# Normalisation of a feed-forward stage's first two groups and four of its first-layer chunks, placed within the last periods of a sixteen-head attention

## The reference

```python
# p 0, 1: x += gate * (gelu(mod(ln(x)) @ W1 + b1) @ W2 + b2), twice
# p 2:    sixteen-head attention
qkv = mod(ln(x)) @ W_qkv                                   # 256 -> 3 * 1024
attn = softmax(q @ k.T / 8)                                # per batch and head, 256 x 256
x = x + g_msa * ((attn @ v) @ W_out + b_out)
# p 3:    feed-forward, hidden width 1024
x = x + g_mlp * (gelu(mod(ln(x)) @ W1 + b1) @ W2 + b2)
# p 4, 5: masked two-direction block and feed-forward;  p 6, 7: one-head attention and feed-forward
```

## Time and profile before

| | before |
|---|---|
| median of three runs | 1716.03 us (1714.61 to 1717.41) |
| the profiled execution | 1716.76 us |
| its span in the trace | 1715.0 us |
| mean granted clock of TensorE | 0.978 |
| busy VectorE, ScalarE, POOL | 73%, 69%, 55% |
| the attention's periods | about 250 to 981 us of the span |

### The profile page before, as it was taken

One profiled execution on the slowest core, in us unless ns is written; L12 is line 12 of the kernel. 1 busy time (PEld: TensorE's weight loads), 2 busy tenths in 40 slices (PEclk: granted clock), 3 DMA queues, 4 the chain that ended last, 5 costly groups with the idle time before them and its releaser, 6 DMA issues.

```text
span 1715.0 us, 37904 instructions
## 1 busy us (share of the span) xinstructions
PE 1623.2 (95%) x13539; PEld 1472.1 (86%) x13539; DVE 1248.6 (73%) x2701; ACT 1181.6 (69%) x2944; POOL 939.8 (55%) x1135
## 2 busy tenths in 40 slices
PE   4888988999999999999999699999999999989997
PEld 2547878999999999999999599998888899979997
DVE  3766857888888888888888655556788778854442
ACT  3545657888888888888888555555766567766663
POOL 1556655666666666666666423233656578832223
PEclk7999998999999999999999899999999999999999
DMA  9223220000000000000000011101212212211111
GB/s 306 56 62 88 75 59 11 9 7 9 10 11 11 11 11 11 11 11 11 11 11 11 16 32 32 32 20 31 61 47 58 53 28 48 47 44 49 32 44 50
DMA packets 110974, 65.96 MB, mean 38 GB/s; under 512 B 81530, under 2 KB 92788, under 8 KB 110788
## 3 DMA queue, kind: packets, MB, share of 16 engines
q1 hardware_dynamic: 110788, 63.54, 14.2%
HBM read 59.06 MB, written 4.46 MB: 37 GB/s over the span
## 4 chain that ended last, share of the span: by engine, by line
PE 82%; DVE 5%; issue 3%; ACT 2%; POOL 1%; DMA 0%; POOLq 0%; DVEq 0%; ACTq 0%
PE bank L290 18%; PE bank L291 16%; PE bank L292 16%; PE bank L1143 7%; PE s_banks L1041 5%; PE bank L1117 4%; PE s_banks L290 4%; PE s_banks L291 4%; PE s_banks L292 4%; PE bank L418 3%; DVE xn L377 2%; DVE vv L1030 1%; PE bank L478 1%; ACT vv L1016 1%; ACT bank L611 0%
## 5 line engine op out<-in xcount | busy, mean ns | idle before, releaser
L1096 POOL TENSOR_TENSOR prob<-prob,rinv 128x512 f32<-128x512 f32 x254 | 259.2, 1041 | 53.0 <-DVE rinv L1077 53.0
L1068 ACT ACTIVATE prob<-s_banks,nmax 128x256 f32<-128x256 f32 x512 | 235.9, 475 | 3.2 <-DVE nmax L1058 3.1
L290 PE MATMUL bank<-WBhi,hl 128*128 128x256 f32 x768 | 218.7, 285 | 5.0 <-DVE upd L648 4.6
L291 PE MATMUL bank<-WBlo,hh 128*128 128x256 f32 x768 | 217.4, 283 | 0.0
L292 PE MATMUL bank<-WBhi,hh 128*128 128x256 f32 x768 | 215.2, 280 | 0.0
L1127 ACT ACTIVATE pthi<-bank 128x512 fp32r<-128x512 f32 x256 | 138.9, 595 | 76.2 <-PE bank L1117 75.7
L611 ACT ACTIVATE hh<-bank,vecs 128x512 fp32r<-128x512 f32 x120 | 82.7, 690 | 156.4 <-PE bank L292 156.3
L1058 DVE TENSOR_REDUCE nmax<-s_banks 128x4 f32<-128x1024 f32 x128 | 156.5, 1222 | 44.8 <-issue 41.0
L431 ACT ACTIVATE nThi<-bank,mod 128x256 fp32r<-128x256 f32 x192 | 110.3, 575 | 106.2 <-issue 76.0
L290 PE MATMUL bank<-aThi,WAlo 128*128 128x256 f32 x576 | 175.3, 304 | 2.6 <-DVE qklo L1025 2.4
L1132 DVE TENSOR_TENSOR ptlo<-bank,pthi 128x512 fp32r<-128x512 f32 x256 | 165.0, 687 | 4.4 <-ACT pthi L1127 0.5
(11 more groups left out here) (185 smaller groups left out, 5733.5 us busy)
## 6 DMA issues: line engine op xcount, KB each, us to landing
gates<-gate_scratch SPq DMA_DIRECT2D x96, 256.0 KB, 3.6
agate<-gate_scratch SPq DMA_DIRECT2D x32, 256.0 KB, 3.7
stage<-in_L_cond_W SPq DMA_DIRECT2D x64, 64.0 KB, 2.3
out<-x SPq DMA_DIRECT2D x16, 256.0 KB, 2.2
adaw<-in_L_cond_Wc SPq DMA_DIRECT2D x1, 3072.0 KB, 17.7
stage<-in_L_cond_W_qkv SPq DMA_DIRECT2D x8, 384.0 KB, 3.4
x<-in_x SPq DMA_DIRECT2D x1, 2560.0 KB, 17.2
stage<-in_L_cond_ff_w SPq DMA_DIRECT2D x32, 64.0 KB, 2.1
```

Of the source, the lines that this page charges most:

```text
L290: pe.matmul(dst, lhs[1], rhs[0], start=start, stop=False, skip_group_check=True)
L291: pe.matmul(dst, lhs[0], rhs[1], start=False, stop=False, skip_group_check=True)
L1068: last = act.activation(prob[h % 4][:, q, :], SB_[h % 2][:, q * SEQ:(q + 1) * SEQ], ACT.Exp, bias=of_head(nmax, h)[:, q:q + 1], accum_out= ...
L1096: pool.tensor_tensor(prob[h % 4][:, :, :], prob[h % 4][:, :, :], scale, ALU.mult).then_inc(prob_ready, 1)
```

## The change

Three things are done. The normalisation of units 0 and 1 leaves j = 3 of the last batch, and that of units 2 and 3 leaves the start of the next stage; all four are spread over periods of the last batch: statistics of units 0 to 3 at j = 1, 2, 5, 6 and the normalising at j = 2, 3, 6, 7. POOL's inverse roots are made unit by unit, behind `o_rest`. And the last period now has four chunks of the next stage's first layer instead of two, for which `ff_body` leaves out chunks 2 and 3 of the first group. A wait for the last exponentials stands ahead of chunk 2, because it writes in the banks of the scores.

```diff
@@ ff_body, TensorE
-                        if nxt:
+                        if nxt and not (first and p == L1_ATTN + 1 and c < HRING - LOOK):
                             ff_hidden(eng, *nxt)
@@ ff_start
-                ff_norms(name, eng, p, g + 1)
+                if p != L1_ATTN + 1:
+                    ff_norms(name, eng, p, g + 1)
@@
         PERIODS = PAIRS * BATCH
+        FF_STATS_AT, FF_NORM_AT = (1, 2, 5, 6), (2, 3, 6, 7)
@@ mh_tensor
             if n == PERIODS - 1:
+                ff_hidden(pe, A + 1, 0, 0, 1)
                 out_pair(pe, n - 2)
                 values_pair(pe, n)
-                ff_hidden(pe, A + 1, 0, 0, 1)
+                pe.wait_ge(exp_ready, HEADS * BATCH)
+                ff_hidden(pe, A + 1, 0, 0, 2)
                 out_pair(pe, n - 1)
+                ff_hidden(pe, A + 1, 0, 0, 3)
                 out_pair(pe, n)
@@ mh_vector
-            if b == BATCH - 1 and j == NEXT - 1:
-                head_norms("vector", dve, A + 1)
+            if b == BATCH - 1 and j in FF_STATS_AT:
+                k = FF_STATS_AT.index(j)
+                ln_stats(dve, A + 1, k, k % GB)
+            if b == BATCH - 1 and j in FF_NORM_AT:
+                k = FF_NORM_AT.index(j)
+                ln_norm(dve, A + 1, k, k % GB)
@@ mh_gpsimd
-            if b == BATCH - 1 and j == NEXT - 1:
-                head_norms("gpsimd", pool, A + 1)
             if n + 1 < PERIODS - SHARED:
                 prob_weigh(pool, 2 * n + 3)
             if n >= 2:
                 o_rest(pool, n - 2, n % 2)
+            if b == BATCH - 1 and j in FF_STATS_AT:
+                k = FF_STATS_AT.index(j)
+                ln_rsqrt(pool, A + 1, k, k % GB)
```

## The result

The changed kernel takes 1705.99 us (1703.74 to 1707.92) where the kernel before takes 1716.44 beside it: ratio 0.9943, 95% interval 0.9932 to 0.9953, so 8.1 to 11.7 us less, and 9.8 by the ratio itself (which isn't the quotient of the two medians; that would be 0.9939, 10.4 us). The prediction was 1704.5 us and -11.5: inside the interval, near its upper end. The profiled execution of after took 1705.73 us with a span of 1703.9 and a mean granted clock of 0.982 (before: 0.978).

The account below looks back on a forecast made before the run. TensorE, at 95% of the span, was taken as the bound, with only its holes and low-clock stretches to win. Batch end -3.3, seam -8.4 and last period +0.2 sum to -11.5 us: 1704.5 us, range 1701.6 to 1709.0.

Parts of the forecast that it names:

- The list of waits as the place to look: End of sixteen-head attention: TensorE's two longest waits, 5.2 us for `prob` and 5.4 for `xn`, are what can be won.
- VectorE as the bound of periods 122 and 123: Batch end: VectorE's slack of 0.76 us a period is gone in period 122, then VectorE sets the periods; gain 3.3 us.
- Normalising beside the weighings: Period 123: unit 1's two `tensor_scalar` beside POOL's weighings cost 1.8 us and end at 950.55; by the lock about 950.85.
- Four waits on POOL at price 0: POOL's inverse roots behind `o_rest` in four periods hold up no transposes: price 0, bound 0.6 us.
- rival 3: Four POOL holds, ending periods 121, 122, 125, 126, each make weighings miss their transposes by 5.15 us: 1723.2 us; chance 0.03.
- The way from the row maxima to period 125, and the periods behind it: Period 124: 3.46 us from `tensor_reduce` to the next period's transposes, so period 125 begins at 954.0 instead of 957.31.
- Rival 2: The low clock moves into period 125 or over the three chunks, costing up to 2.5 us: 1707.0 us; chance 0.10.
- The last period: Chunks 1 to 3 there fill a 1.23 us hole: loss 0.2 us, while two chunks, 2.8 us, leave the next stage.
- The seam: Last projection to fifth chunk's output: 13.1 instead of 21.47 us, gain 8.4, with a new 0.6 us hole ahead of output 3.
- Rival 4: At the seam, the second group's transposes wait as long for something other than `xn`: 1710 us; chance 0.05.
- Rival 1: Moved statistics and normalisations lengthen periods 125 to 127 by the 3.3 us won at the batch end: 1707.8 us; chance 0.12.

Follow-up runs that it names:

- e4_wait_between: The changed kernel with POOL's four inverse roots between its two weighings instead of behind `o_rest`: 1715.11 us, ratio 0.9996 to the kernel before.
- after_again: The changed kernel itself, run again beside three variants: 1705.01 us, ratio 0.9938 to the kernel before.
- e7_fill: The changed kernel plus 11 unused matmuls of 512 columns in period 124, ahead of the value products: 1704.60 us, ratio 0.9936 to the kernel before.
- e1_batch_end: The kernel before with only units 0 and 1 moved (statistics j = 1, 2; normalising j = 2, 3): 1714.53 us, ratio 0.9991 to the kernel before.
- e2_seam_norms: The kernel before with only units 2 and 3 moved (statistics j = 5, 6; normalising j = 6, 7): 1709.89 us, ratio 0.9967 to the kernel before.
- e8_spread_fill: e6_spread plus 4 unused matmuls in period 124 and 6 in period 126, ahead of the value products: 1701.80 us, ratio 0.9916 to the kernel before.
- e10_spread_order: e6_spread with VectorE's `ff_rest` of chunk 3 ahead of the two statistics starting the next stage: 1701.03 us, ratio 0.9917 to the kernel before.
- e5_norm_later: The changed kernel with unit 1 normalised at j = 4 instead of j = 3: 1702.40 us, ratio 0.9935 to the kernel before.
- e6_spread: The changed kernel with units 0 and 1 moved to earlier periods, so no period holds two steps: 1702.87 us, ratio 0.9927 to the kernel before.
- e9_spread_fill_order: e6_spread with both the spare matmuls of e8_spread_fill and the `ff_rest` order of e10_spread_order: 1700.95 us, ratio 0.9919 to the kernel before.

## Why the prediction came out right, and where it did not

*The list of waits as the place to look.* Right: the two waits of the earlier trace rows are gone, and the two parts of the table that held them are shorter by 2.6 + 7.8 = 10.4 us, which includes the two chunks that left the second of them; the two others nearly cancel (1.0 longer, 0.7 shorter).

*VectorE as the bound of periods 122 and 123.* Right nearly to a tenth. With 0.51 us added for the earlier start of period 121, the row maxima of after begin at 937.14, 943.93 and 950.58; the prediction had 937.15, 944.1 and 950.55. The rows of after's VectorE:

```profile
936.63 1.19 DVE L1059 TENSOR_REDUCE nmax<-s_banks 128x4 f32<-128x1024 f32 x1
...
942.20 0.70 DVE L377 TENSOR_SCALAR xn<-x,meanvar,rstd 128x256 f32<-128x256 f32 x2
942.82 0.68 DVE L1199 TENSOR_TENSOR aupd<-bank,agate 128x512 f32<-128x512 f32 x1
943.42 1.22 DVE L1059 TENSOR_REDUCE nmax<-s_banks 128x4 f32<-128x1024 f32 x1
...
948.06 2.09 DVE L377 TENSOR_SCALAR xn<-x,meanvar,rstd 128x256 f32<-128x256 f32 x2
950.07 1.21 DVE L1059 TENSOR_REDUCE nmax<-s_banks 128x4 f32<-128x1024 f32 x1
```

*Normalising beside the weighings.* Unit 0 was undisturbed (0.70 us). For unit 1 the row of before had been read as 0.9 for each `tensor_scalar`, 1.8 in all; it took 2.09, and ended with POOL's second weighing:

```profile
947.91 2.10 POOL L1097 TENSOR_TENSOR prob<-prob,rinv 128x512 f32<-128x512 f32 x2
```

That is the 2.1 that the prediction had worked out beside it by the lock of the Trainium skill's page "SBUF — State Buffer", section "SBUF: two separate sides". The row agrees with the lock: the two VectorE instructions together took as long as the two weighings beside them, three times their 0.70 alone. The step was 0.3 us too low, and VectorE came to it 0.2 us sooner than predicted; that the end was the same is luck.

*Four waits on POOL at price 0.* Right: no wait for `prob` is left in after. e4_wait_between shows that this rested on the place behind `o_rest`; between the weighings the same waits cost 9 us against after, and reached `oTlo` too, which rival 3 had not named. Rival 3's price of 5.15 us for a hold was too high: the four of e4 are 11.8 us in all, 2.9 each, and with them the kernel is as fast as before and not 7.2 us slower. That is the 2.9 us a hold from which the prediction had it slower.

*The way from the row maxima to period 125, and the periods behind it.* This is the step that was mis-sized. The prediction carried 3.46 us over from before; the trace has 954.19 - 950.07 = 4.12, and 10.97 instead of 10.01 for the two periods behind. Up to the value products nothing had changed: they start 2.15 us behind the row maxima in after (952.22) and 2.14 in before:

```profile
955.99 0.36 PE L1143 MATMUL bank<-ptlo,vv 128*128 128x256 f32 x1 [0.58 <-DVE of L1169]
```

From there to period 125 it took 1.32 us in before, where the clock was full again, and 1.97 in after, at 0.50; in after_again, at 1.00, it is 1.32 again. Rival 2 had named the place (a low stretch in period 125 behind the 3 us wait within period 124) and a price of up to 2.5; it cost 0.7 + 1.0 = 1.7 us in this trace and 0.7 in after_again. e7_fill shows that the wait causes it: with the wait filled the low stretch leaves period 125. Periods 125 and 126 go by the clock in the other traces too: 10.97 or 10.98 us at a mean of 0.81 (after, e1_batch_end, e2_seam_norms), 10.65 at 0.84, 10.23 at 0.88 or 0.89, and 10.0 to 10.1 at 0.92 or more; only e4_wait_between, with waits of its own, has 10.37 at 1.00.

*The last period.* The prediction had a loss of 0.2 for the chunks and kept before's low clock there. It came out 0.9 better (12.09 instead of 13.0). In 970 to 975, where the clock of before was 0.73, after has 1.00, and its mean over the whole period is 0.86 where before has 0.79. Why the low stretch was shorter in after isn't shown, and the prediction hadn't reckoned with it: that this made up for half of rival 2's 1.7 us is luck. What the last period has at full clock is 10.87 (e8_spread_fill, whose VectorE has one step less beside it). Thus the bound that the prediction gave for a full clock there (1.2 us of gain) was too small as well; 2.1 was to be had.

*The seam.* The gain was 21.47 - 13.64 = 7.8 instead of 8.4. The predicted new hole of 0.6 us ahead of output 3 is there (0.67, and its end is the statistics, as e10_spread_order shows); the transposes start 1.95 us after the projection instead of 1.8, and the outputs behind a wait take 1.5 instead of 1.42.

*The rivals.* Rival 4 is excluded by the 1.1 us of the list of waits. Rival 1 (the batch end gives its gain back) happened in part: of 3.3 us won e1_batch_end kept 2.2 up to the last projection. Its reason was wrong, since VectorE doesn't lengthen the periods; the clock does: e1_batch_end has none of the moved steps in periods 125 and 126 and takes 10.97 us for them, e5_norm_later has the statistics of units 2 and 3 there and takes 10.01.

The two errors of 1.7 and 0.5 us and the 0.9 in the other direction give 1.3 us in the trace, against an interval of 3.6 us for the measured gain. So the mechanism was right, and that the sum came out this close owes something to errors of both signs.

## What to carry to other kernels

Before a wait on another engine is added to a queue, look at what stands behind it: the same two small POOL instructions cost nothing behind `o_rest` and 9 us between two weighings. A hole of TensorE has two prices, the idle time and the half clock behind it; a smaller hole takes the first away, and the second may come back at the next place where TensorE is busy in pieces, as in e5 and e7. So count the gain over all stretches up to the next dense one, and try a change to the clock in all of them at once.

## What was not expected of the hardware

The low clock needs no single long wait. Already in before the stretch at 0.50 from 966 us on has no wait of over 1.6 us ahead of it since 958. In e5_norm_later and e6_spread the longest wait of the TensorE in 915 to 992 is 1.6 us, and still a stretch at 0.50 (1.2 GHz) follows, behind five microseconds in which TensorE was busy for 2.86 and 3.24. In e8_spread_fill, where spare matmuls stand in two of the gaps, TensorE is busy for 4.53 and 4.20 us ahead of the same place and the clock stays at 1.00 (2.4 GHz). The Trainium skill's page "TensorE: Matmul & The Clock Gate", section "A second HAM failure mode: psum-queue depth-cycling", tells of a kernel in which frequent short idle times between groups of matmuls make the clock swing between its two levels. These traces agree, with waits of 0.2 to 1.6 us between such groups; in e8_spread_fill, where none from 940 to 975 is over 0.6 us, the clock did not fall.

It was also open how far the start of the low stretch is fixed by the kernel. Two traces of the same kernel (after and after_again) have 24.21 and 23.56 us from period 121 to 125 with the same wait of 2.95 and 2.96, since one has the value products behind the wait at half clock and the other has not. The two traces of the spread kernel differ by 0.5 us in the last period in the same way. A difference of this size between single traces need therefore not be an effect of an edit, and what e8_spread_fill and e9_spread_fill_order gain by the clock in every execution stays open.
